# A gated feed-forward kernel in which the router's logits of all four token blocks are computed in one stretch of TensorE instead of two

## The chip, the cores and the metric

The kernel runs on one core of one Trainium2 chip. The metric is the device time of one execution in microseconds (us); the median of the runs is what counts. A core has a matrix engine (TensorE, "PE" in the profile, with its weight loads as "PEld"), a vector engine (VectorE, "DVE"), an activation engine (ScalarE, "ACT"), a general engine (GpSimd, "POOL") and a queue that issues DMAs (SyncE, "SP"). Each engine runs its own instruction list in order; they meet only at semaphores.

## What is computed

The input `x` has 2 x 1024 tokens of 256 channels. A quaternion rotation with a gate (a matrix per lane, folded here into the weights) is applied to it, the result goes through a feed-forward layer with an exact GELU, and the result is scaled by the last expert's softmax probability and added to `x`:

```python
xf = rotate_and_gate(x).reshape(-1, 256)         # linear in x, lane by lane
probs = softmax(xf @ Wr.T, axis=-1)              # 8 experts
h = gelu(xf @ W1[7] + b1[7], approximate=False)  # 256 -> 1024
y = (h @ W2[7] + b2[7]) * probs[:, 7:8]          # 1024 -> 256
return x + y.reshape(x.shape)
```

Everything is float32. Each product of the feed-forward layer is made of three products of a high and a low part (`hi*hi`, `hi*lo`, `lo*hi`).

## The kernel before

The 2048 tokens are four blocks of 512 (`b` = 0 to 3; `LAST` is 3). The hidden layer has eight tiles of 128 (`f` = 0 to 7). On TensorE a block is a loop over `f`: `first_product(b, f)` (six matmuls, L842) makes the input of the GELU, and `turned_product(b, f - 2)` (six matmuls, L865 and L869) multiplies the hidden tile of two steps before with `W2`. The last block's second product is `second_product` (L879 to L887). All orders are written out by hand; no scheduler moves anything.

ScalarE makes for each tile the GELU's high part `h_hi` (L430) and full value `h_all` (L432); VectorE makes the low part `h_lo` (`low_hidden(b, f)`, L599), for which TensorE waits before L869. The next block's `x` is turned by VectorE (`turn_x`, L591, two instructions) and split into high and low by ScalarE (L387) and VectorE (L524).

In block 0 the weights are prepared as well. The last quarter of `W1` (the columns of tiles 6 and 7) is summed on VectorE (`sum_last_w1`, L565 and L570), rounded to its high part on ScalarE (`last_w1_high`, L418), and its low part is made by VectorE (`last_w1_low`, L576). TensorE waits for that low part (`w1_lo_ready`, 3) at the head of `first_product(0, 6)`:

```python
if b == 0 and f % 2 == 0:
    pe.wait_ge(w1_lo_ready, f // 2)
```

The router: `router(pair)` on TensorE (L795) multiplies the turned `x` of two blocks with the router's 32 padded columns. It stands behind `f == 4` of block 0 (for blocks 0 and 1) and behind `f == 4` of block 2 (for blocks 2 and 3). One call issues 16 matmuls in the program, each of which is two in the trace, so 32 loads and 32 matmuls. The logits are turned back and their maximum is taken on VectorE (`logits_of`, L604 and L606), POOL subtracts the maximum (L368) and takes the power (L373, one instruction per block), and VectorE makes the probability (`probability(b)`, L610 to L614). SP spreads it by small DMAs (`spread_prob`), VectorE multiplies the block's turned sums with it (`weigh(b)`, L637; the sums are turned in `turn_sums`, L628) and adds `x` (`add_x(b)`, L649), and SP stores the block. In the last block the probability is used in another form (`bias_and_x`, `add_low`, `add_high`: L655, L660, L666).

Of the kernel before, what the change touches and what calls it, by code (L numbers as in the profile page):

```python
# [9 lines left out]
ALU = mybir.AluOpType  # L10
ACT = mybir.ActivationFunctionType
AX = mybir.AxisListType
# [26 lines left out]
def adaln_ffn(nc, x, small, columns, W1_first, W1_rest, W2, b2, out):  # L39
# [35 lines left out]
    with ExitStack() as ctx:  # L75
# [55 lines left out]
        x_sq = [sb(f"x_sq{b}", [P, SQUARES, LANES]) for b in range(N_BLOCKS)]  # L131
        xT = [sb(f"xT{i}", [P, KC, BLOCK]) for i in range(2)]
        xT_hi = [sb(f"xT_hi{i}", [P, KC, BLOCK], F32R) for i in range(2)]
# [4 lines left out]

        logits_wide = sb("logits_wide", [P, 2 * TT, SQ])
        logits = logits_wide[:, :, 0:NE]  # L140
        logit_max = sb("logit_max", [P, 2 * TT])
        shifted = sb("shifted", [P, 2 * TT, NE])
        e_const = sb("e_const", [P, 1])
        exps = [sb(f"exps{i}", [P, TT, NE]) for i in range(2)]
        exp_sum = sb("exp_sum", [P, TT])
# [4 lines left out]
        yT = sb("yT", [P, KC, BLOCK])  # L150
        y_sq = sb("y_sq", [P, SQUARES, LANES])
        weighed = sb("weighed", [P, SQUARES, LANES])
# [16 lines left out]

        logitsT = lT_bank[:, 0:2 * P].rearrange("p (j t) -> p j t", j=2 * TT)  # L170

# [100 lines left out]
        def _(sp):  # L272
# [42 lines left out]
            load_squares(2)  # L315
            spread_prob(0)
            load_squares(3)
            sp.dma_start(x_last[:, :, :], x_blocks[LAST]).then_inc(last_x_loaded, 16)
            for b in range(LAST):
                if b > 0:  # L320
                    spread_prob(b)
                sp.wait_ge(out_ready, b + 1)
                for q in range(QUADS):
                    rows = out_sq[q * SQ:(q + 1) * SQ, :, :]
                    if b == 0:
                        for h in range(2):
                            sp.dma_start(first_out[h, q], rows[:, h * SQUARES // 2:(h + 1) * SQUARES // 2, :]
                                         ).then_inc(stored, 16)
                    else:
                        sp.dma_start(out_squares[b, q], rows).then_inc(stored, 16)  # L330
# [5 lines left out]
        def _(pool):  # L336
# [18 lines left out]
            for k in range(KC):  # L355
# [9 lines left out]
                                    ALU.add).then_inc(column_M_ready, 1)  # L365
            for pair in range(N_BLOCKS // 2):
                pool.wait_ge(max_ready, pair + 1)
                nc.gpsimd.tensor_tensor(shifted[:, :, :], logits,  # L368
                                        logit_max[:, :].unsqueeze(2).to_broadcast([P, 2 * TT, NE]),
                                        ALU.subtract).then_inc(shifted_ready, 1)  # L370
                pool.wait_ge(shifted_ready, pair + 1)
                for i in range(2):
                    nc.gpsimd.tensor_tensor(exps[i][:, :, :], e_const[:, :].unsqueeze(2).to_broadcast([P, TT, NE]),  # L373
                                            shifted[:, i * TT:(i + 1) * TT, :], ALU.pow).then_inc(exps_ready, 1)

        @block.scalar
        def _(act):
# [6 lines left out]
            def split_x(b, k):  # L384

                act.wait_ge(x_turned, turned(b - 1) + k + 1)
                nc.scalar.activation(xT_hi[b % 2][:, k, :], xT[b % 2][:, k, :], ACT.Copy,  # L387
                                     scale=scale[:, k:k + 1]).then_inc(xT_hi_ready, 1)
# [82 lines left out]
        def _(dve):  # L471
# [50 lines left out]
            def split_x(b, k):  # L522
                dve.wait_ge(xT_hi_ready, KC * (b - 1) + k + 1)
                nc.vector.scalar_tensor_tensor(  # L524
                    out=xT_lo[b % 2][:, k, :], in0=xT[b % 2][:, k, :], scalar=scale[:, k:k + 1],
                    in1=xT_hi[b % 2][:, k, :].bitcast(F32), op0=ALU.mult, op1=ALU.subtract).then_inc(xT_lo_ready, 1)
# [60 lines left out]
            def turn_x(b):  # L587
                dve.wait_ge(x_sq_loaded[b], 16 * QUADS)
                for k in range(KC):

                    nc.vector.transpose(xT[b % 2][:, k, :].rearrange("p (j t s) -> p j s t", j=TT, s=QUADS),  # L591
                                        x_sq[b][:, :, k::KC].rearrange("p (s j) c -> p j s c", j=TT)
                                        ).then_inc(x_turned, 1)
# [7 lines left out]

            def logits_of(pair):
                dve.wait_ge(logitsT_done, pair + 1)
                nc.vector.transpose(logits_wide[:, :, :], logitsT).then_inc(logits_turned, 1)  # L604
                dve.wait_ge(logits_turned, pair + 1)
                nc.vector.tensor_reduce(logit_max[:, :], logits, AX.X, ALU.max).then_inc(max_ready, 1)  # L606

            def probability(b):
                dve.wait_ge(exps_ready, b + 1)
                nc.vector.tensor_reduce(exp_sum[:, :], exps[b % 2][:, :, :], AX.X, ALU.add).then_inc(sum_ready, 1)  # L610
                dve.wait_ge(sum_ready, b + 1)
                nc.vector.reciprocal(inv_sum[:, :], exp_sum[:, :]).then_inc(inv_sum_ready, 1)
                dve.wait_ge(inv_sum_ready, b + 1)
                nc.vector.tensor_tensor(prob[b][:, :], exps[b % 2][:, :, NE - 1], inv_sum[:, :], ALU.mult).then_inc(prob_ready, 1)  # L614
                dve.wait_ge(prob_ready, b + 1)

            def turn_sums(b, k):
                dve.wait_ge(yT_ready, KC * b + k + 1)
                if b > 0:

                    dve.wait_ge(weighed_ready, b)

                n_parts = 2 if b == 0 else 1
                j = TT // n_parts
                for h in range(n_parts):
                    tokens = slice(h * BLOCK // n_parts, (h + 1) * BLOCK // n_parts)
                    rows = slice(h * SQUARES // n_parts, (h + 1) * SQUARES // n_parts)
                    last = nc.vector.transpose(y_sq[:, rows, k::KC].rearrange("p (s j) c -> p j s c", j=j),  # L628
                                               yT[:, k, tokens].rearrange("p (j t s) -> p j s t", j=j, s=QUADS))
                last.then_inc(y_turned, 1)  # L630

            def weigh(b):
                dve.wait_ge(prob_all_loaded[b], 16 * QUADS * (2 if b == 0 else 1))
                dve.wait_ge(y_turned, KC * (b + 1))
                if b > 0:
                    dve.wait_ge(out_ready, b)
                nc.vector.tensor_tensor(weighed[:, :, :], y_sq[:, :, :],  # L637
                                        prob_all[b][:, :].unsqueeze(2).to_broadcast([P, SQUARES, LANES]),
# [55 lines left out]
            for b in range(N_BLOCKS):  # L694
# [6 lines left out]
                if b == 0:  # L701
                    split_w2(1)
                else:
                    turn_sums(b - 1, 1)
                if b == 1:
                    probability(0)
                low_hidden(b, 2)
                if b < LAST:
                    turn_x(b + 1)
                low_hidden(b, 3)  # L710
                if b == 0:
                    sum_last_w1()
                if b == LAST:
                    weigh(b - 1)
                low_hidden(b, 4)
                if b == 0:
                    last_w1_low()
                    split_w2(2)
                if b % 2 == 0:
                    logits_of(b // 2)  # L720
                if b == 0:
                    low_hidden(b, 5)
# [3 lines left out]
                if b == 0:  # L726
                    split_w2(3)
                if b % 2 == 1:
                    probability(b)
                if b == LAST:  # L730
                    add_x(b - 1)
                    bias_and_x(0)
                    bias_and_x(1)
                if b > 0:
                    low_hidden(b, 5)
                if 0 < b < LAST:
                    weigh(b - 1)
                if b == LAST:
                    bias_and_x(2)
                    bias_and_x(3)  # L740
                    last_lows()
                low_hidden(b, 6)
                if 0 < b < LAST:
                    add_x(b - 1)
                if b == 2:
                    probability(b)
                low_hidden(b, 7)
            finish_last()

        @block.tensor  # L750
        def _(pe):
# [27 lines left out]

            def router(pair):  # L780


                if pair == 0:
                    pe.wait_ge(wr_ready, KC)
                    pe.wait_ge(xT_copied, KC)

                    pe.wait_ge(w1_lo_ready, 2)
                else:
                    pe.wait_ge(logits_turned, pair)
                pe.wait_ge(x_turned, turned(2 * pair + 1))  # L790
                for i in range(2):
                    tokens = xT[i][:, :, :].rearrange("p k (j s t) -> p k s j t", j=TT, s=QUADS)
# [133 lines left out]
            for b in range(N_BLOCKS):  # L926
                for f in range(FT):
# [8 lines left out]
                    elif b == LAST and f == SINGLE:  # L936


                        for g in range(f - LAG, SINGLE):
                            second_product(g)  # L940
                    if b % 2 == 0 and f == 4:
                        router(b // 2)
                if b < LAST:
# [49 lines left out]
```

## Time and profile before

| | us |
|---|---|
| median of 3 runs | 103.41 (103.25 to 103.62) |
| the profiled execution, its own time | 103.47 |
| its span from first to last instruction | 101.4 |
| TensorE matmuls busy | 97.7 |
| VectorE busy | 67.2 |
| ScalarE busy | 53.8 |
| GpSimd busy | 28.0 |

The profiled execution took 103.47 us, of which 101.4 us are the span that the profile covers; 2.07 us lie around it. The times in the rows below count from the start of that span. A matmul's row in the trace is longer than the distance to the next one, since matmuls overlap; the distance from start to start is what the engine needs for each.

### The profile page before, as it was taken

The numbers are of one execution on the slowest core, as the hardware profiler recorded it, in microseconds if no ns is written. First come the engines' busy times: TensorE is split into PE (matmuls) and PEld (weight loads), VectorE is DVE, ScalarE is ACT, GpSimd is POOL, SyncE is SP. The second block draws the span as 40 slices with busy tenths as digits, with TensorE's granted clock in tenths as the row PEclk, the third lists the DMA queues.
The fourth block names the chain that finished last, engine by engine and source line by source line (L and its number), as shares of the span: only waits on it lengthen the run. The fifth ranks groups of instructions, "written<-read, shape, count | busy, mean of one in ns | idle before, by whom it ended". The sixth has DMA issues, their size and how long they took to land.

```text
span 101.4 us, 1451 instructions
## 1 busy us (share of the span) xinstructions
PE 97.7 (96%) x516; PEld 81.5 (80%) x516; DVE 67.2 (66%) x131; ACT 53.8 (53%) x89; POOL 28.0 (28%) x21
## 2 busy tenths in 40 slices
PE   6999999999999999999999999999999999999990
PEld 7679888778888888888888888788888888888980
DVE  1579689999940789486623695466922666599551
ACT  1467695854434955774408944854408944453600
POOL 3300054001999950000000000089998000000000
PEclk9999999999999999999999999999999999999999
DMA  2999999991000000129334100000054000007105
GB/s 65 311 246 250 209 221 214 222 187 25 0 0 0 0 6 1 5 54 211 150 84 99 26 1 0 6 0 0 0 119 90 1 0 0 6 5 176 26 20 187
DMA packets 20246, 8.17 MB, mean 81 GB/s; under 512 B 17808, under 2 KB 18704, under 8 KB 20240
## 3 DMA queue, kind: packets, MB, share of 16 engines
q1 hardware_dynamic: 19520, 7.30, 34.6%
q10 hardware_dynamic: 720, 0.79, 2.4%
q8 instruction: 4, 0.07, 0.3%
q14 instruction: 2, 0.02, 0.1%
HBM read 5.97 MB, written 2.10 MB: 80 GB/s over the span
## 4 chain that ended last, share of the span: by engine, by line
PE 93%; DMA 2%; DVE 2%; DVEq 0%; issue 0%
PE pre L842 41%; PE acc L865 21%; PE acc L869 11%; PE acc L879 4%; PE acc L887 4%; PE pre L806 3%; PE acc L761 2%; PE lT_bank L795 2%; DMA quats<-in_small 2%; PE acc L883 1%; PE acc L881 1%; DVE y L666 1%; PE acc L777 1%; PE lT_bank L777 1%; DVEq L75 0%; PE acc L771 0%
## 5 line engine op out<-in xcount | busy, mean ns | idle before, releaser
L430 ACT ACTIVATE h_hi<-pre,quats 128x512 fp32r<-128x512 f32 x32 | 22.1, 690 | 36.1 <-PE pre L842 33.9
L599 DVE TENSOR_TENSOR h_lo<-h_all,h_hi 128x512 fp32r<-128x512 f32 x32 | 22.0, 688 | 25.7 <-ACT h_all L432 25.7
L865 PE MATMUL acc<-h_hi,w_parts 128*128 128x512 f32 x96 | 25.7, 389 | 0.0
L842 PE MATMUL pre<-xT_hi,w_hi 128*128 128x512 f32 x60 | 23.6, 394 | 0.0
L842 PE MATMUL pre<-xT_lo,w_hi 128*128 128x512 f32 x60 | 23.4, 391 | 0.0
L373 POOL TENSOR_TENSOR exps<-e_const,shifted 128x32 f32<-128x32 f32 x4 | 22.3, 5580 | 0.2
L432 ACT ACTIVATE h_all<-pre,quats 128x512 f32<-128x512 f32 x32 | 21.9, 684 | 0.0
L865 PEld LDWEIGHTS acc<-h_hi,w_parts 128*128 128x128 f32 x96 | 18.0, 188 | 3.7
L842 PE MATMUL pre<-xT_hi,w_lo 128*128 128x512 f32 x60 | 18.5, 390 | 0.0
L869 PE MATMUL acc<-h_lo,w_parts 128*128 128x512 f32 x48 | 14.8, 389 | 0.0
L842 PEld LDWEIGHTS pre<-xT_hi,w_hi 128*128 128x128 f32 x60 | 11.3, 188 | 2.6 <-issue 0.4
L842 PEld LDWEIGHTS pre<-xT_hi,w_lo 128*128 128x128 f32 x60 | 11.3, 188 | 2.4
L842 PEld LDWEIGHTS pre<-xT_lo,w_hi 128*128 128x128 f32 x60 | 11.3, 188 | 2.1
L368 POOL TENSOR_TENSOR shifted<-logits_wide,logit_max 128x64 f32<-128x64 f32 x2 | 1.4, 702 | 38.0 <-DVE logit_max L606 38.0
L869 PEld LDWEIGHTS acc<-h_lo,w_parts 128*128 128x128 f32 x48 | 9.0, 188 | 1.9
L628 DVE STREAM_TRANSPOSE y_sq<-yT 128x256 f32<-128x256 f32 (+1 forms) x8 | 6.8, 868 | 0.3
L887 PE MATMUL acc<-w_parts,h_lo 128*128 128x256 f32 x32 | 6.1, 282 | 0.0
L591 DVE STREAM_TRANSPOSE xT<-x_sq 128x512 f32<-128x512 f32 x6 | 6.0, 1082 | 0.0
L887 PEld LDWEIGHTS acc<-w_parts,h_lo 128*128 128x128 f32 x32 | 5.1, 190 | 0.4
L879 PE MATMUL acc<-w_parts,h_hi 128*128 128x512 f32 x20 | 5.4, 390 | 0.0
L524 DVE SCALAR_TENSOR_TENSOR xT_lo<-xT,scale,xT_hi 128x512 fp32r<-128x512 f32 x6 | 4.3, 757 | 0.0
L879 PEld LDWEIGHTS acc<-w_parts,h_hi 128*128 128x128 f32 x20 | 3.7, 188 | 0.7
(87 smaller groups left out, 87.6 us busy)
## 6 DMA issues: line engine op xcount, KB each, us to landing
x_sq<-in_x SPq DMA_DIRECT2D x12, 128.0 KB, 4.5
w<-in_W SPq DMA_DIRECT2D x4, 256.0 KB, 6.4
w_last<-in_W_rest SPq DMA_DIRECT2D x4, 256.0 KB, 5.6
out<-out_sq SPq DMA_DIRECT2D x8, 128.0 KB, 2.7
x_sq<-in_x SPq DMA_DIRECT2D x8, 64.0 KB, 5.3
x_last<-in_x SPq DMA_DIRECT2D x1, 512.0 KB, 3.9
out<-out_sq SPq DMA_DIRECT2D x8, 64.0 KB, 2.2
w_first<-in_W_first ACTq DMA_DIRECT2D x2, 132.0 KB, 2.8
```

The lines of the kernel that those rows point to most:

```text
L373: nc.gpsimd.tensor_tensor(exps[i][:, :, :], e_const[:, :].unsqueeze(2).to_broadcast([P, TT, NE]), shifted[:, i * TT:(i + 1) * TT, :], ALU. ...
L430: nc.scalar.activation(h_hi[:, s, :], pre_bank(b, f)[:, :], ACT.Gelu, bias=b1_cols[:, f:f + 1]).then_inc(h_hi_ready, 1)
L432: nc.scalar.activation(h_all[:, s, :], pre_bank(b, f)[:, :], ACT.Gelu, bias=b1_cols[:, f:f + 1]).then_inc(h_ready, 1)
L524: nc.vector.scalar_tensor_tensor(out=xT_lo[b % 2][:, k, :], in0=xT[b % 2][:, k, :], scalar=scale[:, k:k + 1], in1=xT_hi[b % 2][:, k, :].bi ...
L591: nc.vector.transpose(xT[b % 2][:, k, :].rearrange("p (j t s) -> p j s t", j=TT, s=QUADS), x_sq[b][:, :, k::KC].rearrange("p (s j) c -> p ...
L599: nc.vector.tensor_tensor(h_lo[:, s, :], h_all[:, s, :], h_hi[:, s, :].bitcast(F32), ALU.subtract).then_inc(h_lo_ready, 1)
L628: last = nc.vector.transpose(y_sq[:, rows, k::KC].rearrange("p (s j) c -> p j s c", j=j), yT[:, k, tokens].rearrange("p (j t s) -> p j s t ...
L842: last = nc.tensor.matmul(bank[:, :], w[:, k, cols], part_of_x[:, k, :], start=(n == 0), stop=(n == len(steps) - 1))
L865: nc.tensor.matmul(sums(b, k), w2_parts[:, f, i, k * P:(k + 1) * P], h_hi[:, s, :], start=(f == 0 and i == 0), stop=False)
L869: last = nc.tensor.matmul(sums(b, k), w2_parts[:, f, 0, k * P:(k + 1) * P], h_lo[:, s, :], start=False, stop=(f == FT - 1))
L879: nc.tensor.matmul(acc[j][:, :], rows, w2_parts[:, f, :, :], start=(f == 0), stop=False)
L887: return nc.tensor.matmul(acc_high[j], h_lo[:, f % SLOTS, j * P:(j + 1) * P], w2_parts[:, f, 0, :], start=False, stop=(f in (SINGLE - 1, F ...
```

## The change

All four blocks' logits are computed in one call of `router()`, which stands behind `f == 5` of block 1. For that the turned `x` of all blocks is kept (four buffers instead of two), and block 3's `x` is turned already in block 1. The logits are turned back and reduced once, for all blocks; POOL subtracts once and then takes the power four times. `weigh` and `add_x` of blocks 0 and 1 both stand in block 2 now (`y_sq` gets a second buffer), those of block 2 stand one step earlier in block 3, and all four probabilities are made by the end of block 2. SP issues the loads of block 3's `x` and of `x_last` before it waits for the first probability.

The diff, cut to its core:

```diff
@@ tiles @@
-        xT = [sb(f"xT{i}", [P, KC, BLOCK]) for i in range(2)]
+        xT = [sb(f"xT{b}", [P, KC, BLOCK]) for b in range(N_BLOCKS)]
...
-        y_sq = sb("y_sq", [P, SQUARES, LANES])
+        y_sq = [sb(f"y_sq{i}", [P, SQUARES, LANES]) for i in range(2)]
@@ SP @@
             load_squares(2)
-            spread_prob(0)
             load_squares(3)
             sp.dma_start(x_last[:, :, :], x_blocks[LAST]).then_inc(last_x_loaded, 16)
+            spread_prob(0)
             for b in range(LAST):
-                if b > 0:
-                    spread_prob(b)
+                if b + 1 < LAST:
+                    spread_prob(b + 1)
@@ POOL @@
-            for pair in range(N_BLOCKS // 2):
-                pool.wait_ge(max_ready, pair + 1)
...
+            pool.wait_ge(max_ready, 1)
...
+            for b in range(N_BLOCKS):
+                nc.gpsimd.tensor_tensor(exps[b][:, :, :], e_const[:, :].unsqueeze(2).to_broadcast([P, TT, NE]),
+                                        shifted[:, b * TT:(b + 1) * TT, :], ALU.pow).then_inc(exps_ready, 1)
@@ DVE, turn_sums @@
-                if b > 0:
-                    dve.wait_ge(weighed_ready, b)
+                if b > 1:
+                    dve.wait_ge(weighed_ready, b - 1)
@@ DVE, the loop over blocks @@
-                if b == 1:
-                    probability(0)
                 low_hidden(b, 2)
...
+                if b == 1:
+                    turn_x(LAST)
+                if b == 2:
+                    weigh(0)
...
-                if b % 2 == 0:
-                    logits_of(b // 2)
...
+                if b == 1:
+                    all_logits()
+                if b == 2:
+                    weigh(1)
...
                 low_hidden(b, 7)
+                if b == 1:
+                    probability(0)
+                if b == 2:
+                    add_x(1)
@@ PE @@
-                    if b % 2 == 0 and f == 4:
-                        router(b // 2)
+                    if b == 1 and f == 5:
+                        router()
```

How the instructions stand on TensorE in block 0, from the second product of tile 2 to the first products of tile 5. Before:

```order
L865 MATMUL acc1<-h_hi,w2_parts 128x512 x2
L869 MATMUL acc0<-h_lo,w2_parts 128x512
L869 MATMUL acc1<-h_lo,w2_parts 128x512
L795 MATMUL lT_bank<-xT0,wr_wide 32x128 x8
L795 MATMUL lT_bank<-xT1,wr_wide 32x128 x8
L842 MATMUL pre2<-xT_hi0,w1_hi 128x512
L842 MATMUL pre2<-xT_lo0,w1_hi 128x512
```

The same place on TensorE now:

```order
L868 MATMUL acc1<-h_hi,w2_parts 128x512 x2
L872 MATMUL acc0<-h_lo,w2_parts 128x512
L872 MATMUL acc1<-h_lo,w2_parts 128x512
L845 MATMUL pre2<-xT_hi0,w1_hi 128x512
L845 MATMUL pre2<-xT_lo0,w1_hi 128x512
```

The router's matmuls are gone from there: what follows them, the first products of tiles 5 and 6, comes directly behind the second product of tile 2.

On TensorE in block 1, between the second product of tile 3 and the first product of tile 6, where no router stood before, stands now:

```order
L872 MATMUL acc2<-h_lo,w2_parts 128x512
L872 MATMUL acc3<-h_lo,w2_parts 128x512
L798 MATMUL lT_bank<-xT0,wr_wide 32x128 x8
L798 MATMUL lT_bank<-xT1,wr_wide 32x128 x8
L798 MATMUL lT_bank<-xT2,wr_wide 32x128 x8
L798 MATMUL lT_bank<-xT3,wr_wide 32x128 x8
L845 MATMUL pre2<-xT_hi1,w1_hi 128x512
```

All 32 of the program's router matmuls (64 in the trace) follow each other there.

On VectorE in block 0, from the sum of the last quarter of `W1` to the split of block 1's `x`. Before:

```order
L565 TENSOR_SCALAR w1_last_sum<-w1_last,column_M 128x256 x2
L570 SCALAR_TENSOR_TENSOR w1_last_sum<-w1_last,column_M,w1_last_sum 128x256 x6
L599 TENSOR_TENSOR h_lo<-h_all,h_hi 128x512
L576 TENSOR_TENSOR w1_lo<-w1_last_sum,w1_hi 128x2x256
L582 CAST w2_parts<-w2 128x2x256
L584 TENSOR_TENSOR w2_parts<-w2,w2_parts 128x2x256
L604 STREAM_TRANSPOSE logits_wide<-lT_bank 128x256
L606 TENSOR_REDUCE logit_max<-logits_wide 128x8
L599 TENSOR_TENSOR h_lo<-h_all,h_hi 128x512
```

The same place on VectorE now:

```order
L564 TENSOR_SCALAR w1_last_sum<-w1_last,column_M 128x256 x2
L569 SCALAR_TENSOR_TENSOR w1_last_sum<-w1_last,column_M,w1_last_sum 128x256 x6
L598 TENSOR_TENSOR h_lo<-h_all,h_hi 128x512
L575 TENSOR_TENSOR w1_lo<-w1_last_sum,w1_hi 128x2x256
L581 CAST w2_parts<-w2 128x2x256
L583 TENSOR_TENSOR w2_parts<-w2,w2_parts 128x2x256
L598 TENSOR_TENSOR h_lo<-h_all,h_hi 128x512
```

The two instructions of the logits have left; what stands ahead of the low part of `W1`'s last quarter is the same as before.

## Rows read from the trace of the kernel before

**Rows 1.** The page: busy time and share of each engine; granted clock in 40 slices.

```profile
PE 97.7 (96%) x516; PEld 81.5 (80%) x516; DVE 67.2 (66%) x131; ACT 53.8 (53%) x89; POOL 28.0 (28%) x21
...
PEclk9999999999999999999999999999999999999999
```

**Rows 2.** Who waited for whom: us in total, times, longest.

```profile
PE lT_bank L754 <- PEq L986: 0.8, 1, 0.8
```

**Rows 3.** The chain that ended last, around both routers: start us, us, what.

```profile
16.83 1.36 PE pre L842 x6
...
19.55 1.01 PE lT_bank L795 x32
20.56 1.58 PE pre L842 x6
...
64.31 1.01 PE lT_bank L795 x32
65.32 1.58 PE pre L842 x6
```

**Rows 4.** Matmuls in time, 19 to 25 us: start us, us, engine line op.

```profile
20.49 0.50 PE L842 MATMUL pre<-xT_hi,w_hi 128*128 128x512 f32 x1
...
21.98 1.07 PE L865 MATMUL acc<-h_hi,w_parts 128*128 128x512 f32 x4
...
23.34 0.39 PE L842 MATMUL pre<-xT_hi,w_hi 128*128 128x512 f32 x1
...
24.70 1.07 PE L865 MATMUL acc<-h_hi,w_parts 128*128 128x512 f32 x4
```

**Rows 5.** Weight loads and matmuls, 19 to 24 us and around 68 us.

```profile
19.48 0.81 PEld L795 LDWEIGHTS lT_bank<-xT,wr_wide 128*32 128x32 f32 x32 [0.35 <-issue]
...
23.20 0.19 PEld L842 LDWEIGHTS pre<-xT_hi,w_hi 128*128 128x128 f32 x1
...
67.88 0.19 PEld L842 LDWEIGHTS pre<-xT_hi,w_hi 128*128 128x128 f32 x1
68.10 0.39 PE L842 MATMUL pre<-xT_hi,w_hi 128*128 128x512 f32 x1
```

**Rows 6.** VectorE (and ScalarE's L418) in time, block 0.

```profile
13.86 0.69 DVE L599 TENSOR_TENSOR h_lo<-h_all,h_hi 128x512 fp32r<-128x512 f32 x1 [0.35 <-ACT h_all L432]
...
19.29 2.46 DVE L570 SCALAR_TENSOR_TENSOR w_last_sum<-w_last,column_M,w_last_sum 128x256 f32<-128x256 f32 x6
21.67 0.69 DVE L599 TENSOR_TENSOR h_lo<-h_all,h_hi 128x512 fp32r<-128x512 f32 x1
21.79 0.63 ACT L418 ACTIVATE w_hi<-w_last_sum 128x512 fp32r<-128x512 f32 x1 [1.08 <-DVE w_last_sum L570]
22.46 0.69 DVE L576 TENSOR_TENSOR w_lo<-w_last_sum,w_hi 128x512 fp32r<-128x512 f32 x1
```

**Rows 7.** The chain that ended last, in the opening: start us, us, what.

```profile
9.45 1.91 PE pre L806 x16
```

**Rows 8.** In time, blocks 1 and 2, where the moved work will stand.

```profile
38.62 2.02 DVE L591 STREAM_TRANSPOSE xT<-x_sq 128x512 f32<-128x512 f32 x2
40.47 0.69 DVE L599 TENSOR_TENSOR h_lo<-h_all,h_hi 128x512 fp32r<-128x512 f32 x1
...
45.10 0.39 PE L842 MATMUL pre<-xT_hi,w_hi 128*128 128x512 f32 x1
...
54.77 0.69 DVE L599 TENSOR_TENSOR h_lo<-h_all,h_hi 128x512 fp32r<-128x512 f32 x1 [3.39 <-ACT h_all L432]
...
58.25 0.62 PE L869 MATMUL acc<-h_lo,w_parts 128*128 128x512 f32 x2
```

**Rows 9.** Groups: line, engine, operation, count | busy us, mean ns | idle before.

```profile
L373 POOL TENSOR_TENSOR exps<-e_const,shifted 128x32 f32<-128x32 f32 x4 | 22.3, 5580 | 0.2
...
L368 POOL TENSOR_TENSOR shifted<-logits_wide,logit_max 128x64 f32<-128x64 f32 x2 | 1.4, 702 | 38.0 <-DVE logit_max L606 38.0
...
L604 DVE STREAM_TRANSPOSE logits_wide<-lT_bank 128x256 f32<-128x256 f32 x2 | 0.9, 446 | 0.4 <-PE lT_bank L795 0.4
```

More of the change, by code:

```diff
@@ L137, in adaln_ffn @@
         h_lo = sb("h_lo", [P, SLOTS, BLOCK], F32R)
-        logits_wide = sb("logits_wide", [P, 2 * TT, SQ])
+        logits_wide = sb("logits_wide", [P, N_BLOCKS * TT, SQ])
         logits = logits_wide[:, :, 0:NE]
-        logit_max = sb("logit_max", [P, 2 * TT])
-        shifted = sb("shifted", [P, 2 * TT, NE])
+        logit_max = sb("logit_max", [P, N_BLOCKS * TT])
+        shifted = sb("shifted", [P, N_BLOCKS * TT, NE])
         e_const = sb("e_const", [P, 1])
-        exps = [sb(f"exps{i}", [P, TT, NE]) for i in range(2)]
+        exps = [sb(f"exps{b}", [P, TT, NE]) for b in range(N_BLOCKS)]
         exp_sum = sb("exp_sum", [P, TT])
@@ L168, in adaln_ffn @@
         lT_bank = ctx.enter_context(nc.psum_tensor("lT_bank", [P, 512], F32))
-        logitsT = lT_bank[:, 0:2 * P].rearrange("p (j t) -> p j t", j=2 * TT)
+        logitsT = lT_bank[:, :].rearrange("p (j t) -> p j t", j=N_BLOCKS * TT)
         xT_ps = [bank[:, 0:HALF] for bank in (acc[2], pre[2])]
@@ L365, in _ @@
                                     ALU.add).then_inc(column_M_ready, 1)
-            for pair in range(N_BLOCKS // 2):
-                pool.wait_ge(max_ready, pair + 1)
[L368 to L374, printed above, removed]
+            pool.wait_ge(max_ready, 1)
+            nc.gpsimd.tensor_tensor(shifted[:, :, :], logits,
+                                    logit_max[:, :].unsqueeze(2).to_broadcast([P, N_BLOCKS * TT, NE]),
+                                    ALU.subtract).then_inc(shifted_ready, 1)
+            pool.wait_ge(shifted_ready, 1)
+            for b in range(N_BLOCKS):
+                nc.gpsimd.tensor_tensor(exps[b][:, :, :], e_const[:, :].unsqueeze(2).to_broadcast([P, TT, NE]),
+                                        shifted[:, b * TT:(b + 1) * TT, :], ALU.pow).then_inc(exps_ready, 1)
         @block.scalar
@@ L386, in split_x @@
                 act.wait_ge(x_turned, turned(b - 1) + k + 1)
-                nc.scalar.activation(xT_hi[b % 2][:, k, :], xT[b % 2][:, k, :], ACT.Copy,
+                nc.scalar.activation(xT_hi[b % 2][:, k, :], xT[b][:, k, :], ACT.Copy,
                                      scale=scale[:, k:k + 1]).then_inc(xT_hi_ready, 1)
@@ L524, in split_x @@
                 nc.vector.scalar_tensor_tensor(
-                    out=xT_lo[b % 2][:, k, :], in0=xT[b % 2][:, k, :], scalar=scale[:, k:k + 1],
+                    out=xT_lo[b % 2][:, k, :], in0=xT[b][:, k, :], scalar=scale[:, k:k + 1],
                     in1=xT_hi[b % 2][:, k, :].bitcast(F32), op0=ALU.mult, op1=ALU.subtract).then_inc(xT_lo_ready, 1)
@@ L589, in turn_x @@
                 for k in range(KC):
-                    nc.vector.transpose(xT[b % 2][:, k, :].rearrange("p (j t s) -> p j s t", j=TT, s=QUADS),
+                    nc.vector.transpose(xT[b][:, k, :].rearrange("p (j t s) -> p j s t", j=TT, s=QUADS),
                                         x_sq[b][:, :, k::KC].rearrange("p (s j) c -> p j s c", j=TT)
@@ L600, in low_hidden, with all_logits @@
                                         ALU.subtract).then_inc(h_lo_ready, 1)
-            def logits_of(pair):
-                dve.wait_ge(logitsT_done, pair + 1)
+            def all_logits():
+                dve.wait_ge(logitsT_done, 1)
                 nc.vector.transpose(logits_wide[:, :, :], logitsT).then_inc(logits_turned, 1)
-                dve.wait_ge(logits_turned, pair + 1)
+                dve.wait_ge(logits_turned, 1)
                 nc.vector.tensor_reduce(logit_max[:, :], logits, AX.X, ALU.max).then_inc(max_ready, 1)
@@ L609, in probability @@
                 dve.wait_ge(exps_ready, b + 1)
-                nc.vector.tensor_reduce(exp_sum[:, :], exps[b % 2][:, :, :], AX.X, ALU.add).then_inc(sum_ready, 1)
+                nc.vector.tensor_reduce(exp_sum[:, :], exps[b][:, :, :], AX.X, ALU.add).then_inc(sum_ready, 1)
                 dve.wait_ge(sum_ready, b + 1)
@@ L613, in probability @@
                 dve.wait_ge(inv_sum_ready, b + 1)
-                nc.vector.tensor_tensor(prob[b][:, :], exps[b % 2][:, :, NE - 1], inv_sum[:, :], ALU.mult).then_inc(prob_ready, 1)
+                nc.vector.tensor_tensor(prob[b][:, :], exps[b][:, :, NE - 1], inv_sum[:, :], ALU.mult).then_inc(prob_ready, 1)
                 dve.wait_ge(prob_ready, b + 1)
@@ L627, in turn_sums @@
                     rows = slice(h * SQUARES // n_parts, (h + 1) * SQUARES // n_parts)
-                    last = nc.vector.transpose(y_sq[:, rows, k::KC].rearrange("p (s j) c -> p j s c", j=j),
+                    last = nc.vector.transpose(y_sq[b % 2][:, rows, k::KC].rearrange("p (s j) c -> p j s c", j=j),
                                                yT[:, k, tokens].rearrange("p (j t s) -> p j s t", j=j, s=QUADS))
@@ L636, in weigh @@
                     dve.wait_ge(out_ready, b)
-                nc.vector.tensor_tensor(weighed[:, :, :], y_sq[:, :, :],
+                nc.vector.tensor_tensor(weighed[:, :, :], y_sq[b % 2][:, :, :],
                                         prob_all[b][:, :].unsqueeze(2).to_broadcast([P, SQUARES, LANES]),
@@ L704, in _ @@
                     turn_sums(b - 1, 1)
+                low_hidden(b, 2)
+                if b == 0:
+                    turn_x(1)
                 if b == 1:
-                    probability(0)
-                low_hidden(b, 2)
-                if b < LAST:
-                    turn_x(b + 1)
+                    turn_x(2)
+                if b == 2:
+                    probability(1)
+                if b == LAST:
+                    weigh(2)
                 low_hidden(b, 3)
@@ L712, in _ @@
                     sum_last_w1()
+                if b == 1:
+                    turn_x(LAST)
+                if b == 2:
+                    weigh(0)
                 if b == LAST:
-                    weigh(b - 1)
+                    add_x(2)
                 low_hidden(b, 4)
@@ L718, in _ @@
                     split_w2(2)
-                if b % 2 == 0:
-                    logits_of(b // 2)
-                if b == 0:
                     low_hidden(b, 5)
@@ L727, in _ @@
                     split_w2(3)
-                if b % 2 == 1:
-                    probability(b)
+                if b == 2:
+                    probability(2)
+                    add_x(0)
                 if b == LAST:
-                    add_x(b - 1)
-                    bias_and_x(0)
-                    bias_and_x(1)
+                    for j in range(TT):
+                        bias_and_x(j)
                 if b > 0:
                     low_hidden(b, 5)
-                if 0 < b < LAST:
-                    weigh(b - 1)
+                if b == 1:
+                    all_logits()
+                if b == 2:
+                    weigh(1)
                 if b == LAST:
-                    bias_and_x(2)
-                    bias_and_x(3)
                     last_lows()
                 low_hidden(b, 6)
-                if 0 < b < LAST:
-                    add_x(b - 1)
                 if b == 2:
-                    probability(b)
+                    probability(LAST)
                 low_hidden(b, 7)
+                if b == 1:
+                    probability(0)
+                if b == 2:
+                    add_x(1)
             finish_last()
@@ L778, in fold, with router @@
                                      start=True, stop=True).then_inc(folded, 1)
[L780 to L791, printed above, removed]
+            def router():
+                pe.wait_ge(wr_ready, KC)
+                pe.wait_ge(xT_copied, KC)
+                pe.wait_ge(w1_lo_ready, 2)
+                pe.wait_ge(x_turned, turned(LAST))
+                for i in range(N_BLOCKS):
                     tokens = xT[i][:, :, :].rearrange("p k (j s t) -> p k s j t", j=TT, s=QUADS)
```

## The prediction, made before the change was run

> **What bounds the kernel now.** I read the busy shares first. TensorE is busy in 97.7 of 101.4 us and its granted clock is full in all slices, the other engines stand well below it [rows 1]. Then who waited for whom: the longest wait that TensorE's matmuls have in the whole program is 0.8 us, at its very start [rows 2]; from 11 us on no matmul waits for another engine. The chain that ended last is TensorE's own instruction list, piece after piece [rows 3]. So the time is the sum of TensorE's steps, and two questions decide: what does the change take from that list or put into it, and does TensorE, once it is earlier or later against the others, meet a wait that it doesn't meet today?
>
> In the chain a first product takes 1.36 us; the one behind the router takes 1.58 us, and the router's 32 matmuls take 1.01 us [rows 3]. One router call so costs 1.01 + 0.22 = 1.23 us: the work, and a restart of the wide matmuls behind it. The second call, in block 2, reads the same, 1.01 and 1.58 us.
>
> **Part 1: the call in block 0 goes.** TensorE's list is 1.23 us shorter there. The next wait decides what is left of it. The first product of tile 6 starts at 23.34 us [rows 4], and it needs the low part of the last quarter of `W1`. VectorE finishes that (L576) at 22.46 + 0.69 = 23.15 us [rows 6]. The weight load of that product starts at 23.20 us, 0.05 us behind it and only 0.14 us ahead of its matmul; an undisturbed one, in block 2, starts 0.22 us ahead, at 67.88 for 68.10 us [rows 5]. So this load already waits for VectorE today, by some 0.08 us, and no row of waits shows it, since the matmul ahead is still running. TensorE has no slack here.
>
> Without the router the matmul would start at 23.34 - 1.23 = 22.11 us, unless the low part comes earlier as well. Can it? Going back from L576: it follows ScalarE's L418 (21.79 to 22.42 us), which follows the last L570 (19.29 + 2.46 = 21.75 us), and VectorE runs without an idle time since 13.86 us, where it had waited for a GELU of tile 1 [rows 6]. All that lies ahead of the router, and the instructions ahead of L576 are the same after the change. The two logit instructions that leave VectorE stand behind L576. ScalarE's L418 stands ahead of the next GELU, so an earlier first product doesn't disturb it either. So the load can start at 23.20 us at the earliest, TensorE idles about 1.1 us and restarts. For the restart I take the one behind the router: from 20.49 to 21.98 us, 1.49 us until the second product [rows 4]. That puts the second product of tile 4 at 23.20 + 1.49 = 24.69 us; today it starts at 24.70 us [rows 4]. Gain: 0.01 us of the 1.23. **The wait takes the router's place.**
>
> **Part 2: one call of 64 in block 1.** It has the same restart, 0.22 us, and the first 32 matmuls, 1.01 us. For 32 more the rows bound the price from 0.81 us (32 weight loads from the first start to the last end [rows 5]) to 1.01 us (the whole event again [rows 3]); neither a saving below 0.81 nor a gain is possible, since nothing of the 32 is left out. I take 0.9, between the two, because the 1.01 holds one way in and out. Cost: 1.23 + 0.9 = 2.13 us. TensorE must not wait for block 3's turned `x` in front of it. VectorE ends the low part of tile 3 at 40.47 + 0.69 = 41.16 us, without `probability(0)` ahead of it about 0.5 us earlier, then turns `x` in 2.02 us [rows 8]: done by 43.2 us at the latest, and the router's place is at 45.10 us [rows 8]. Cover 1.9 us.
>
> **Part 3: the call in block 2 goes.** Its 1.23 us are gained if nothing is late there, now that the other steps are 2.1 us later. What TensorE needs in block 2 is bound by TensorE itself: VectorE waited 3.39 us for tile 0's GELU [rows 8]. I take all 1.23.
>
> **Part 4: the moved softmax and weighing, beside TensorE.** The router ends about 47.2 us; turning twice the columns takes about 0.9 us (twice 0.45 [rows 9]) and the maximum, I estimate, half of that; POOL's subtraction 1.4 us at most (twice 0.70), the first power 5.6 us [rows 9]. The first probability is so made at about 56.2 us. Behind it on VectorE's list stands tile 0 of block 2, which can start at 54.77 + 2.1 = 56.9 us, so the new wait ends 0.7 us ahead of it; and TensorE asks for it only at 58.25 + 2.1 = 60.3 us [rows 8], another 2.8 us. The four powers take 22.3 us [rows 9] and end at about 72 us, about when block 2 asks for the last. SP's loads of block 3's `x` and of `x_last` move to about 21 us, behind all loads that block 0 needs, so they delay none of them. The two `weigh` and two `add_x` that now stand in block 2 were there before as well, one pair a block earlier, and VectorE is busy in only two thirds of the span [rows 1]. Price on the path: 0.
>
> **The sum**, against the profiled execution's 103.47 us: -0.01 (block 0) + 2.13 (block 1) - 1.23 (block 2) = +0.89 us, so 104.36 us. That execution lies 0.06 us above the median of the runs, so 104.3 us as a median. The tail behind TensorE's last matmul doesn't change.
>
> **The rivals.**
>
> *The gain in block 0 stays (faster).* If the low part of `W1` came by 22.1 us, the sum would be -1.23 + 2.13 - 1.23 = -0.33 us: 103.1 us. Against it stands VectorE's unbroken list. It decides in parts: each tenth by which L576 ends earlier than 23.15 us gives a tenth back, and from about 0.9 us earlier the kernel is no slower than before.
>
> *The long call runs out of queued instructions (slower still).* Ahead of a router call TensorE's matmuls need 1.36 us for six [rows 3], 227 ns each, so its 32 pairs can be queued before they run; of 64 pairs the later ones may come at the pace at which they are fed. The rows show that 32 run at about 27 ns each (0.81 to 1.01 us); how fast pairs are fed without a stock they don't show. The slowest dense small pairs are the opening's, 16 in 1.91 us, 119 ns each [rows 7], which would make the second 32 cost 3.8 instead of 0.9 us: 107.2 us; the fast end is the forecast. For it speaks that no stretch of over 32 such pairs exists; against it that the two calls run evenly to their last matmul. The Trainium skill ("TensorE: Matmul & The Clock Gate", Part 1, on the gap of 56 ns, and its table) says that the queue holds 64 instructions, and that a matmul costs about 62 ns in the sequencer where the decoding in hardware is off. By that rule 32 pairs fit the queue, which agrees with the rows, and the 32 others would take 2.0 instead of 0.9 us, an estimate of 105.4 us.
>
> *VectorE piles up in block 2.* A probability that comes late holds `weigh(0)`, and the low parts behind it. It decides only where a low part is more than about 2.8 us late, since that is how long block 2's first lies ready before its use (55.46 to 58.25 us [rows 8]); from there each us is a us: 105 to 106 us for one or two of them.
>
> *Something of the 0.89 us is hidden* by an effect that the rows don't show, and the result is within the measurement.
>
> **How the numbers follow.** Forecast (slower by 0.8 to 1.0 us) 0.80; the gain in block 0 stays, wholly or mostly, 0.07; long call fed slowly 0.08; pile-up 0.03; hidden 0.02. A measurement of this kernel tells about 0.3%, 0.31 us, from no change. The first rival lies just at that bound, so I give it half and half: faster 0.04, within 0.06 with the hidden case rounded up, slower 0.90. The range holds the forecast with both ends of the second 32's price, the spread of the runs (0.2 us to either side), a third of block 0's gain at the low end, and the milder half of the slow feeding at the high end: 103.9 to 105.1 us.
>
> **What would show it.** Block 0: TensorE idle about 1.1 us ahead of the first product of tile 6, released by VectorE's L575 line (L576 before), which still ends near 23.15 us; the second product of tile 4 near 24.7 us. Block 1: 64 router matmuls in 1.8 to 2.0 us, the 33rd to 64th at the distance of the first. Block 2: first products all 1.36 us in the chain, none 1.58. Everything behind about 67 us later by 0.9 us. The prediction is wrong if L576's line ends clearly earlier, if the router's matmuls spread out in their second half, or if a wait for a low part (`h_lo`) ends TensorE's idle time in block 2 or 3.

## The result, and the profile after

The changed kernel takes 104.11 us (median of 6 runs, 103.79 to 104.74), the kernel before 103.26 us in the runs beside it. The ratio is 1.0091, with a 95% interval of 1.0053 to 1.0130: slower, by about 0.9 us. A second set of 12 runs on another occasion gave 104.03 against 103.40 us, ratio 1.0064 (1.0038 to 1.0089). The forecast was 104.3 us and +0.89 us. (Medians in this document are over all executions of a kernel, while the ratios leave out the few that were over 1.5% slower than its fastest, so a ratio can differ a little from the quotient of the medians.)

The two profiled executions differ by only 0.32 us (103.79 and 103.47 us), because the opening, which the change doesn't touch, was 0.43 us shorter in the one after. The first loads landed at about the same time in both; what differs is that the first four matmuls on weights (L761, L767 after) took 2.10 us of the chain before and 1.40 us after, and why is not shown. Over all profiles of this case tile 2's first product starts between 10.6 and 11.4 us. So traces are compared here from that product's start to the start of the last matmul. Matmuls in time, the kernel before (start us, us, engine line op):

```profile
11.20 0.40 PE L842 MATMUL pre<-xT_hi,w_hi 128*128 128x512 f32 x1
...
98.38 0.28 PE L887 MATMUL acc<-w_parts,h_lo 128*128 128x256 f32 x1
```

and the changed kernel:

```profile
10.77 0.40 PE L845 MATMUL pre<-xT_hi,w_hi 128*128 128x512 f32 x1
...
98.69 0.28 PE L890 MATMUL acc<-w_parts,h_lo 128*128 128x256 f32 x1
```

That is 87.18 us before and 87.92 us after, +0.74 us. (This stretch is called "the body" below; the tail behind it is 3.0 to 3.1 us in every profile.) Its pieces can be read off one by one. First who waited for whom in the changed kernel; TensorE had no such row before [rows 2]:

```profile
PEld pre L845 <- DVE w_lo L575: 1.2, 1, 1.2
...
PE pre L845 <- DVE w_lo L575: 0.8, 1, 0.8
```

The chain that ended last has left TensorE in block 0. Before, it was TensorE's own pieces there, the router among them [rows 3]; now it goes through VectorE and ScalarE (start us, us, what):

```profile
17.59 0.67 DVE h_lo L598
18.27 0.52 DVE w_last_sum L564 x2
18.79 2.39 DVE w_last_sum L569 x6
...
21.20 0.64 ACT w_hi L417
...
21.86 0.70 DVE w_lo L575
...
22.61 1.67 PE pre L845 x6
24.28 0.93 PE acc L868 x4
```

and the only router call, in block 1, shows in the same chain as

```profile
44.70 1.88 PE lT_bank L798 x64
46.59 1.58 PE pre L845 x6
```

Matmuls and weight loads in time around tile 6 of block 0, the changed kernel, beside [rows 4] and [rows 5]:

```profile
21.22 0.61 PE L872 MATMUL acc<-h_lo,w_parts 128*128 128x512 f32 x2
22.61 0.50 PE L845 MATMUL pre<-xT_hi,w_hi 128*128 128x512 f32 x1 [0.77 <-DVE w_lo L575]
...
24.12 1.09 PE L868 MATMUL acc<-h_hi,w_parts 128*128 128x512 f32 x4
...
22.61 0.19 PEld L845 LDWEIGHTS pre<-xT_hi,w_hi 128*128 128x128 f32 x1 [1.19 <-DVE w_lo L575]
```

The load of tile 6's first product starts 0.06 us behind the end of L575 (21.86 + 0.69 = 22.55 us), as it did before (0.05 us behind 23.15 us, [rows 5, 6]). Before, the wait lay hidden under the running matmul; now it is bare. The waits view calls it 0.8 us for the matmuls, since it counts from the modelled end of the matmul ahead; from start to start the gap is 1.16 us, of which 0.23 us is the usual distance, so 0.93 us are lost. With the slower restart behind it (1.51 instead of 1.36 us until the second product, 0.15 us) that makes 1.08 us in the place of the router's 1.23 us.

### The profile page after: what moved, and what is told of

The parts are those of the page before. It is cut to its first block, busy times and chain, and to the rows that moved or that the text cites. A ratio compares the mean times of both kernels' runs of the same rounds, so it can differ in the third digit from the quotient of the medians.

```text
span 101.7 us, 1445 instructions
## 1 busy us (share of the span) xinstructions
PE 97.1 (95%) x516; PEld 81.2 (80%) x516; DVE 66.9 (66%) x129; ACT 53.9 (53%) x89; POOL 26.9 (26%) x20
## 4 chain that ended last, share of the span: by engine, by line
PE 81%; DVE 10%; ACT 4%; DMA 2%; issue 1%; DVEq 0%
PE pre L845 35%; PE acc L868 18%; PE acc L872 9%; PE acc L882 4%; PE acc L890 4%; PE pre L809 3%; DVE w_last_sum L569 2%; DMA quats<-in_small 2%; DVE h_lo L598 2%; PE lT_bank L798 2%; DVE xT L590 2%; PE acc L767 1%; ACT h_hi L429 1%; PE acc L886 1%; PE acc L884 1%; ACT h_all L431 1%
## 5 line engine op out<-in xcount | busy, mean ns | idle before, releaser
L431 ACT ACTIVATE h_all<-pre,quats 128x512 f32<-128x512 f32 x32 | 21.9, 684 | 0.0
L648 DVE TENSOR_TENSOR out_sq<-weighed,x_sq 128x1024 f32<-128x1024 f32 x3 | 3.7, 1223 | 1.8 <-DMA out<-out_sq 1.8
```

The source lines that it names most:

```text
L431: nc.scalar.activation(h_all[:, s, :], pre_bank(b, f)[:, :], ACT.Gelu, bias=b1_cols[:, f:f + 1]).then_inc(h_ready, 1)
L648: nc.vector.tensor_tensor(out_sq[:, :, :], weighed[:, :, :], x_sq[b][:, :, :], ALU.add).then_inc(out_ready, 1)
```

## The experiments

Each row of the table is a kernel that is told of below, with its body from its own profile.

| kernel | median us | ratio to before (95%) | body us |
|---|---|---|---|
| before | 103.4 | 1 | 87.18 |
| changed | 104.11, 104.03 | 1.0091, 1.0064 | 87.92, 87.88 |
| blocks 0 and 1 back in block 0 | 103.48 | 0.9994 (0.9964 to 1.0025) | 87.17 |
| before, block 0's call behind tile 6 | 104.82 | 1.0123 (1.0059 to 1.0187) | 88.50 |
| changed, call issued twice | 106.14 | 1.0240 (1.0178 to 1.0301) | 89.68 |
| changed, call cut in two | 104.41 | 1.0103 (1.0067 to 1.0140) | 88.29 |
| changed, sum of `W1` first | 104.27 | 1.0048 (1.0007 to 1.0088) | 88.21 |
| the same, its load first too | 102.77 | 0.9943 (0.9917 to 0.9969) | 86.81 |

The theory (A): the router's call in block 0 was free, because it ran in a stretch that TensorE would otherwise have waited for the low part of `W1`'s last quarter. Its rivals: the moved softmax, weighings and loads cost the time (B), or the one long call does (C).

### Half of the router back in block 0

```diff
-                    if b == 1 and f == 5:
-                        router()
+                    if b == 0 and f == 4:
+                        router((0, 1))
+                    if b == 1 and f == 5:
+                        router((2, 3))
```

> The changed kernel with one thing undone: the logits of blocks 0 and 1 are computed in block 0 again, behind tile 4, as before; those of blocks 2 and 3 stay in block 1. Everything else (softmax, weighings, loads) stays as changed. Theory A (the router in block 0 cost nothing, because TensorE has to wait for the low part of W1's last quarter anyway, and the moved softmax and weighings cost nothing beside TensorE): -0.9 us against the changed kernel, the same as the kernel before within 0.1 us (ratio 1.000), no idle time of TensorE ahead of tile 6's first product, one router event of 1.23 us in block 1. Theory B (the loss comes from the moved work on VectorE, POOL or SP): stays near 104.1 us, ratio 1.009. Theory C (the loss comes from one long call): the two short calls cost 2 x 1.23 us on the path, 104.3 us or more if none is hidden.

Measured: ratio 0.9994, body 87.17 us, 0.01 us from the kernel before. Its chain has both short events, 1.01 and 1.58 us each, and no wait at tile 6:

```profile
19.60 1.01 PE lT_bank L798 x32
20.61 1.58 PE pre L846 x6
...
45.31 1.01 PE lT_bank L798 x32
46.32 1.58 PE pre L846 x6
```

All the rest of the change is in this kernel: four powers in a row on POOL, two weighings in block 2, the earlier loads. They cost nothing. B is out: whatever those moved steps cost is under the noise. One call moved from block 2 to block 1 costs nothing either; only the one that leaves block 0 does.

### The kernel before with its call behind tile 6

```diff
-                    if b % 2 == 0 and f == 4:
-                        router(b // 2)
+                    if b == 0 and f == 6:
+                        router(0)
+                    if b == 2 and f == 4:
+                        router(1)
```

On VectorE `logits_of(0)` is moved behind `split_w2(3)`, to stand behind the router.

> The kernel before with its block 0 router call moved from behind tile 4 to behind tile 6, behind the product that waits for W1's low part; as many instructions on every engine. Theory A: TensorE waits about 1.1 us ahead of tile 6 as in the changed kernel, and pays the router's 1.23 us behind it in full: +1.2 us against the kernel before, ratio 1.012. If the router's place didn't matter, ratio 1.000.

Measured: ratio 1.0123, body +1.32 us, with as many instructions as before. The chain shows the wait through VectorE first and the router behind it:

```profile
21.90 0.70 DVE w_lo L576
...
22.65 1.67 PE pre L843 x6
24.32 0.93 PE acc L866 x4
...
25.70 1.01 PE lT_bank L796 x32
```

This is the clearest form of A: behind the wait the call costs its full 1.23 us, while two places further up nearly all of it is covered by the wait. The remaining 0.07 us lie ahead of the call: tile 4's second product starts 13.57 us behind tile 2's first (24.16 - 10.59) instead of 13.50 us.

### The long call issued twice

```diff
                     if b == 1 and f == 5:
                         router()
+                        router()
```

VectorE waits for the second call.

> The changed kernel with the router call of block 1 issued twice in a row, 128 matmuls instead of 64; the second computes the same logits again. Theory A (a steady 27 ns for each pair of load and matmul, at any length): +1.75 us against the changed kernel, 105.9 us, ratio 1.025 to the kernel before. Slow feeding once the queued instructions are used up: the groups spread from some place on, +3 to +4 us at 60 ns for a pair.

Measured: ratio 1.024, 106.14 us, body +1.76 us against the changed kernel's 87.92 us. The call in the chain, and the matmuls' own row (ns min/median/max, first and last start us):

```profile
45.33 3.63 PE lT_bank L798 x128
...
L798 PE MATMUL lT_bank<-xT,wr_wide x128: 272/273/297, 45.3 to 48.7; 128*32 128x128 f32 x128
```

64 matmuls more cost 3.63 - 1.88 = 1.75 us, 27.3 ns each, as the second half of the first 64 did (1.88 - 1.01 = 0.87 us for 32). They come evenly: in the stretches of 0.7 us that begin at 46.0, 46.7 and 47.4 us the trace has 35, 36 and 36 matmuls under way. So the rival of the prediction that the queue runs dry is out, up to 128 pairs. The figure of about 62 ns for each matmul that the Trainium skill ("TensorE: Matmul & The Clock Gate", Part 1) names for the case that the decoding in hardware is off didn't show: 128 at 62 ns would be 7.9 us. Counted by the program's 64 matmuls, each of which is two in the trace, it would be 4.0 us, an estimate that is nearer but still above the measured 3.63 us.

### The long call cut in two

```diff
-                    if b == 1 and f == 5:
-                        router()
+                    if b == 1 and f == 5:
+                        router((0, 1))
+                    if b == 1 and f == 6:
+                        router((2, 3))
```

> The changed kernel with its call of 64 router matmuls cut into two calls of 32 in block 1, behind tile 5 and behind tile 6. Theory A (each event costs 0.36 us for the way in and out, beside 0.87 us for 32 matmuls): +0.36 us against the changed kernel, ratio 1.012 to 1.013 to the kernel before; in the trace two events of 1.23 us. If an event had no fixed cost, +0.0 us.

Measured: body +0.37 us against the changed kernel (+0.41 us against the profile of it that was taken beside this one), ratio 1.0103. The ratio is a little under the expected 1.012 to 1.013, which its interval just covers; the body is as expected. The chain has the two events (start us, us, what):

```profile
44.59 1.01 PE lT_bank L798 x32
45.60 1.58 PE pre L846 x6
...
48.55 1.01 PE lT_bank L798 x32
49.56 1.58 PE pre L846 x6
```

The way in and out of a call costs 0.36 us on its own; that is what merging two calls saves. It also answers C: the long call costs less (2.10 us) than the two short ones (2.46 us). Where all of them lie on the path, merging is a gain.

### The sum of W1's last quarter ahead of turning x

If A holds, an earlier low part gives the time back. Block 0, VectorE, and the same on ScalarE (`last_w1_high` ahead of `split_x`, which moves behind tile 5's GELU):

```diff
                 low_hidden(b, 2)
                 if b == 0:
-                    turn_x(1)
+                    sum_last_w1()
...
-                if b == 0:
-                    sum_last_w1()
...
                     last_w1_low()
                     split_w2(2)
+                    turn_x(1)
                     low_hidden(b, 5)
+                    split_w2(3)
...
-                if b == 0:
-                    split_w2(3)
```

> The changed kernel with another order in block 0: VectorE sums W1's last quarter and makes its low part, and splits W2's third part, ahead of turning block 1's x; ScalarE rounds the sum ahead of splitting block 1's x. Theory A (the wait for that low part is what ate the gain in block 0): the low part is ready about 1.5 to 2 us earlier, TensorE's idle time of about 1.1 us ahead of tile 6 goes, less 0.1 to 0.4 us if a W2 part comes late instead: 103.1 to 103.3 us, 0.7 to 1.0 us under the changed kernel, at or slightly under the kernel before (ratio 0.996 to 1.000). If the wait were only a symptom of something else (W2's parts, turned x), TensorE would idle as long at a later product of block 0, and the time stays at 104.1 us.

Measured: 104.27 us, ratio 1.0048. This expectation was missed: no gain that could be told from the changed kernel, and the body is 0.29 us longer. Who waited for whom names the reason:

```profile
DVE w_last_sum L564 <- DMA w_last<-in_W_rest: 2.1, 1, 2.1
...
PEld pre L843 <- DVE w_lo L575: 0.9, 1, 0.9
PEld acc L870 <- DVE h_lo L598: 0.9, 2, 0.6
```

The sum now stood first on VectorE's list, but its data, the last of `W1`'s loads, were not there (the chain that ended last; start us, us, what):

```profile
11.07 7.04 DMA w_last<-in_W_rest
18.20 0.62 DVE w_last_sum L564 x2
```

The load landed at 11.07 + 7.04 = 18.11 us, and VectorE stood 2.1 us behind it. So the sum started only 0.27 us earlier than in the changed kernel, counted from tile 2's first product (18.20 - 11.04 = 7.16 instead of 18.20 - 10.77 = 7.43 us). In this order the low parts of two tiles (3 and 4) stand between the sum and the low part of `W1`, instead of one, which takes that back and more. Besides, a low part of the hidden tiles came late for TensorE at the end of block 0 (a row of 0.56 instead of 0.45 us in the chain). The executions of this kernel also scatter most, from 103.08 to 107.05 us; that would fit a time that hangs on when a load lands, but it isn't shown.

I had read the unbroken VectorE list as the only reason for the low part's time; the load was right behind it. The trace shows when VectorE's queue got past its wait for the load (the instruction at L563 before, L562 after; ns, then first and last start in us). Before, and in the changed kernel:

```profile
L563 DVEq EVENT_SEMAPHORE  x1: 21/21/21, 18.7 to 18.7; - x1
...
L562 DVEq EVENT_SEMAPHORE  x1: 21/21/21, 17.5 to 17.5; - x1
```

So in the profile of the kernel before the sum did wait for the load: L599 ends at 18.69 us and L565 starts 0.07 us behind that. In the changed kernel's profile the load was there 0.7 us ahead, and the same pair overlaps by 0.06 us. VectorE in time, before:

```profile
18.02 0.67 DVE L599 TENSOR_TENSOR h_lo<-h_all,h_hi 128x512 fp32r<-128x512 f32 x1
18.76 0.62 DVE L565 TENSOR_SCALAR w_last_sum<-w_last,column_M 128x256 f32<-128x256 f32 x2
```

and after:

```profile
17.59 0.67 DVE L598 TENSOR_TENSOR h_lo<-h_all,h_hi 128x512 fp32r<-128x512 f32 x1
18.20 0.59 DVE L564 TENSOR_SCALAR w_last_sum<-w_last,column_M 128x256 f32<-128x256 f32 x2
```

### The load first too

To the kernel above, on SP:

```diff
             load_w2(1)
-            load_squares(1)
             sp.dma_start(column_quats[:, :], columns).then_inc(columns_loaded, 16)
...
             load_w2(2)
+            load_squares(1)
             load_w2(3)
```

The loads of `W1`'s last quarter so stand ahead of those of block 1's `x`.

> The kernel of the second run (the sum of W1's last quarter ahead of turning block 1's x), with the loads of W1's last quarter issued ahead of the loads of block 1's x. In the second run VectorE waited 2.1 us for that load, so the order gained little. Theory A, with the load as the second cause of the same wait: the sum starts about 16.1 us instead of 18.2 us, the low part is ready by about 21 us, TensorE runs without idle time past tile 6, and the time is 103.0 to 103.2 us, ratio 0.995 to 0.998 to the kernel before (-0.36 us) and 1.1 us under the changed kernel. If something else holds TensorE in block 0, an idle time of similar length shows at another product and the ratio stays over 1.003.

Measured: 102.77 us, ratio 0.9943 (0.9917 to 0.9969), faster than both kernels. The body is 86.81 us: 0.37 us under the kernel before, which is the saving of the merged call (0.36 us), and 1.11 us under the changed kernel. The medians differ by more, 0.63 us; the interval of the ratio (0.3 to 0.9 us) holds both. VectorE's queue got past its wait for the load at 15.7 us. VectorE in time, and TensorE's matmuls at tile 6:

```profile
16.17 0.61 DVE L564 TENSOR_SCALAR w_last_sum<-w_last,column_M 128x256 f32<-128x256 f32 x2
...
20.27 0.69 DVE L575 TENSOR_TENSOR w_lo<-w_last_sum,w_hi 128x512 fp32r<-128x512 f32 x1
...
21.68 0.62 PE L870 MATMUL acc<-h_lo,w_parts 128*128 128x512 f32 x2
22.14 0.39 PE L843 MATMUL pre<-xT_hi,w_hi 128*128 128x512 f32 x1
```

The low part is ready at 20.96 us and is wanted at about 21.9 us; there is about 1 us of slack where there had been none, and no wait of TensorE is left in block 0. Two things held the sum near 18.2 us, VectorE's order and, close behind it, the load. The order alone gained nothing; the load alone was not tried.

## Why the prediction was right, point by point

- **What bounds the kernel.** Right: TensorE's list is the time, and each difference in a body is one of its pieces or its one wait, at tile 6.
- **The call in block 0.** Said: 1.23 us off, 1.1 us of idle time and a restart in its place, gain 0.01 us. Measured: 0.93 us idle, and from tile 2's start to the second product of tile 4 it is 24.12 - 10.77 = 13.35 us after and 24.70 - 11.20 = 13.50 us before, a gain of 0.15 us. The mechanism was right; the term was 0.14 us too high. Of that, 0.13 us lie at the start of the sum: 7.56 us behind tile 2's first product before (18.76 - 11.20), 7.43 us after. The prediction called VectorE's list unbroken since 13.86 us; it had this one hole, the wait for the load, and the rows that were chosen left it out. The hole belongs to the execution and not to the kernel: the wait for the load ended between 17.5 and 18.8 us in the profiles in which the load's place is unchanged. Without a router in block 0 a load that lands behind VectorE's other work delays TensorE, so the forecast took one execution's late load for a part of the kernel.
- **The restart.** Said 1.49 us until the second product, measured 24.12 - 22.61 = 1.51 us.
- **The call of 64.** Said 2.13 us, measured 1.88 + 0.22 = 2.10 us in the chain; the second 32 cost 0.87 us where 0.9 was taken.
- **The call in block 2.** All of its 1.23 us were gained: every first product of block 2 is a piece of 1.36 us.
- **The moved work.** Said 0 on the path: shown by the kernel with half of the router back. Its working had one size wrong and left one wait out. The first power ended at 53.7, not 55.6 us: POOL's subtraction took 0.4 instead of at most 1.4 us, the router ended 0.6 us earlier than assumed, and turning and the maximum were a little shorter. So VectorE stood idle for 2.06 us between the probability and block 2's first tile, where 0.7 us had been expected. And `add_x(1)` had to wait for block 0's stores, which now come late in block 2. VectorE in time, after:

```profile
53.72 0.19 DVE L609 TENSOR_REDUCE exp_sum<-exps 128x4 f32<-128x32 f32 x1 [0.80 <-POOL exps L372]
...
56.38 0.69 DVE L598 TENSOR_TENSOR h_lo<-h_all,h_hi 128x512 fp32r<-128x512 f32 x1 [2.06 <-ACT h_all L431]
...
76.54 1.23 DVE L648 TENSOR_TENSOR out_sq<-weighed,x_sq 128x1024 f32<-128x1024 f32 x1 [1.79 <-DMA out<-out_sq]
78.07 0.69 DVE L598 TENSOR_TENSOR h_lo<-h_all,h_hi 128x512 fp32r<-128x512 f32 x1 [0.31 <-ACT h_all L431]
```

  The addition behind that wait ended 0.3 us before block 3's first low part could start, and TensorE's first matmul on that low part starts at 81.56 us, 2.8 us behind its end (78.07 + 0.69 us). It cost nothing, with a cover of about 3.1 us, but it should have been in the sum's list of hidden things.
- **The rivals.** The gain in block 0 would stay if the low part came early: the last experiment made it come early, and the body then was 0.37 us under the kernel before, where the prediction had computed 0.33 us. The slow feeding of a long call is excluded up to 128 pairs. The pile-up in block 2 didn't occur.
- **The sum.** Body +0.74 us in the profiles against +0.89 us said; the measured terms give -0.15 + 2.10 - 1.23 = +0.72 us. The medians give +0.85 and +0.63 us. That the first of them meets the forecast to 0.04 us is in part luck: two sets of executions differ by more than that, and the body says that the forecast was 0.15 us too high.

## What to carry to other kernels

On an engine that is busy all the time, an instruction's price is not its duration: ask which wait comes next behind it, and read that wait where it is hidden, from the distance between a weight load and its matmul or from how close the releaser's end is to the load's start, not from the table of waits. Work that sits in front of such a wait is nearly free (1.23 us of it were worth 0.15 us here), and taking it out and paying for it elsewhere is a loss, however much cheaper the merged form is. When the wait itself is to be moved, look for the second thing that is late by nearly the same amount (here a load behind the order on VectorE), and move both.

## What the hardware showed that I had not expected

- Four loads and matmuls of 32 columns on four parts of the array keep a pace of 109 ns for each group of four (27.3 ns each) for as long as 128 of them follow each other; into and out of such a stretch TensorE loses 0.36 us beside the usual distances.
- POOL's subtraction of 128x128 elements took 404 ns, while that of 128x64 took 673 and 732 ns in the kernel before [rows 9], so half the data took longer. The record points to the work beside it. In six profiles POOL subtracts once for all blocks while VectorE is idle, and takes 404 or 405 ns each time. With the call cut in two, the same subtraction of 128x128 falls beside VectorE's making of a low part and takes 789 ns:

```profile
50.58 0.68 DVE L598 TENSOR_TENSOR h_lo<-h_all,h_hi 128x512 fp32r<-128x512 f32 x1
50.74 0.79 POOL L367 TENSOR_TENSOR shifted<-logits_wide,logit_max 128x128 f32<-128x128 f32 x1 [34.97 <-DVE logit_max L605]
```

  In the kernel before, both subtractions stand beside VectorE's work as well: the first, at 24.91 us, beside L599 (24.74 us, 0.68 us), the second, at 66.17 us, beside L524 (66.00 us, 1.44 us for two). What the two engines share there isn't shown.

- VectorE's transposition of all logits, 128x512, took 0.72 us, where 128x256 took 0.45 us [rows 9]: 0.8 of the time for each element.
